# The global term of a fused attention kernel: one split-precision matmul of 96 rows, or a plain fp32 matmul of 32 rows

## The reference

```python
h = einsum('bhid,oi,od->bho', x, weighted_sum, weight)    # (4, 512, 256)
h = concatenate([h, txt], axis=1)                         # (4, 589, 256): 77 rows of text
n = layernorm(h)
gate = sigmoid(relu(n @ gate_w1 + gate_b1) @ gate_w2 + gate_b2)   # 64, then R = 32 columns
glob = gate * (n @ U_w) * cumsum(n @ V_w, axis=1)                 # (4, 589, 32)
h = h + conv3(n, conv_w) + glob @ out_w + out_b                   # out_w is 32 x 256
# then layernorm again, both operands rounded to 8-bit integers, their product, scaled, added to h
```

## Time and profile before

| | before |
|---|---|
| time, median of 3 runs | 128.95 us |
| time of the profiled execution | 129.47 us |
| its span, first to last instruction | 127.7 us |
| PE busy | 109.4 us (86%) |
| DVE busy | 88.2 us (69%) |
| ACT busy | 59.3 us (46%) |
| POOL busy | 49.5 us (39%) |
| mean granted TensorE clock | 0.967 |

### The profile page before, as it was taken

The page is one execution under the profiler, slowest core; times in us unless marked ns, Lnnn a source line. Parts: engine busy times, 40 slices in busy tenths (PEclk is TensorE's granted clock), DMA queues, the critical chain, the costliest instruction groups (busy, mean ns, idle before and its releaser), DMA issues.

```text
span 127.7 us, 1866 instructions
## 1 busy us (share of the span) xinstructions
PE 109.4 (86%) x568; PEld 88.3 (69%) x568; DVE 88.2 (69%) x266; ACT 59.3 (46%) x128; POOL 49.5 (39%) x91
## 2 busy tenths in 40 slices
PE   6169999999999999999979999998995389199960
PEld 6057886687886988788658868866882277099740
DVE  0251440659519688975978898599689999978962
ACT  4000037564632584747247582934485846315520
POOL 2000042002202437171637646360947437416840
PEclk9999999999999999999999999999999959968997
DMA  2999999992000000000022000002020001300014
GB/s 86 253 362 285 397 417 424 424 421 85 0 0 0 0 0 0 8 0 0 0 82 81 1 27 5 0 0 85 0 82 25 0 0 41 124 5 25 0 41 148
DMA packets 5447, 12.55 MB, mean 98 GB/s; under 512 B 471, under 2 KB 3391, under 8 KB 4671
## 3 DMA queue, kind: packets, MB, share of 16 engines
q1 hardware_dynamic: 5151, 11.93, 25.9%
q10 hardware_dynamic: 288, 0.52, 1.4%
HBM read 10.04 MB, written 2.41 MB: 98 GB/s over the span
## 4 chain that ended last, share of the span: by engine, by line
PE 58%; DVE 21%; DMA 8%; issue 3%; ACT 3%; SPq 2%; POOL 2%; DVEq 0%; POOLq 0%
PE h_ps L708 31%; DMA txt_sb<-txt_dram 8%; DVE convT L603 6%; DVE csum L591 5%; PE uvg_ps L766 5%; PE h_ps L790 4%; PE xt_ps L824 3%; PE qt_ps L806 3%; DVE stats L542 3%; DVE tmp L669 3%; PE acc_ps L817 2%; PE h_ps L793 2%; SPq L299 2%; PE xt_ps L752 2%; PE uvg_ps L773 2%
## 5 line engine op out<-in xcount | busy, mean ns | idle before, releaser
L708 PE MATMUL h_ps<-w_tok,x_sb 128*128 128x256 f32 x256 | 64.6, 396 | 3.9 <-DVE w_tok L537 3.9
L708 PEld LDWEIGHTS h_ps<-w_tok,x_sb 128*128 128x128 f32 x256 | 48.3, 198 | 13.1 <-DMA x_sb<-x_dram 4.2
L542 DVE BATCH_NORM_STATS2 stats<-h_ps 128x6 f32<-128x256 f32 (+1 forms) x36 | 13.9, 422 | 12.0 <-PE h_ps L793 6.6
L340 POOL TENSOR_SCALAR rstd<-mv 128x2 f32<-128x2 f32 (+2 forms) x21 | 4.7, 226 | 40.5 <-DVE mv L545 40.0
L378 POOL TENSOR_SCALAR v<-xc,qmul 128x256 f32<-128x256 f32 (+1 forms) x20 | 10.7, 540 | 16.6 <-DVE qmul L647 16.4
L603 DVE SCALAR_TENSOR_TENSOR convT<-xnT,par_sb,convT 128x255 f32<-128x255 f32 (+1 forms) x32 | 16.4, 567 | 0.0
L341 POOL TENSOR_TENSOR rstd<-rstd,exponent 128x2 f32<-128x2 f32 (+2 forms) x21 | 14.9, 711 | 1.7
L494 ACT ACTIVATE xc<-h_ps,nmean 128x256 f32<-128x256 f32 (+1 forms) x20 | 8.6, 469 | 10.7 <-DVE nmean L619 10.7
L470 ACT ACTIVATE glob<-glob 32x256 fp32r<-32x256 f32 (+1 forms) x16 | 7.2, 448 | 11.9 <-POOL glob L352 6.3
L484 ACT ACTIVATE xn<-h_ps,shift,rstd 128x256 f32<-128x256 f32 x16 | 8.2, 563 | 8.7 <-DVE shift L631 8.6
L352 POOL TENSOR_TENSOR glob<-gate,us 32x256 f32<-32x256 f32 x8 | 6.6, 830 | 13.6 <-ACT gate L461 13.6
(11 more groups left out here) (75 smaller groups left out, 141.0 us busy)
## 6 DMA issues: line engine op xcount, KB each, us to landing
x_sb<-x_dram SPq DMA_DIRECT2D x6, 1024.0 KB, 17.2
out_dram<-fin SPq DMA_DIRECT2D x8, 256.0 KB
x_sb<-x_dram SPq DMA_DIRECT2D x4, 256.0 KB, 6.5
x_sb<-x_dram SPq DMA_DIRECT2D x2, 512.0 KB, 9.8
wt_sb<-wt_dram ACTq DMA_DIRECT2D x2, 256.0 KB, 4.7
txt_sb<-txt_dram SPq DMA_DIRECT2D x1, 308.0 KB
out_dram<-fin SPq DMA_DIRECT2D x4, 77.0 KB
par_sb<-par_dram SPq DMA_DIRECT2D x1, 277.0 KB, 10.6
```

The source lines that it names most:

```text
L542: last = nc.vector.bn_stats(stats[0:rows, t, :], src(t))
L708: last = nc.tensor.matmul(h_of(g)[:, t, :], x_sb[:, g, kc, t * P:(t + 1) * P], w_tok[:, kc, :], start=(kc == 0 and t == 0), stop=(kc == KC ...
```

## The change

The matmul of the global term reads `glob` and `outw` as they are, fp32, 32 rows. The rounded copies, the subtraction, both buffers, the type and three semaphores go. `mix` waits for `glob` itself, and GpSimd's wait before it overwrites `glob` is now for the `mix` that read it.

```diff
-        glob3 = sb("glob3", [3 * R, 2, L], F32R)
-        outw3 = sb("outw3", [3 * R, D], F32R)
...
             def gated(g):
                 b, half = divmod(g, HALVES)
                 if half == 0 and b >= 2:
-                    pool.wait_ge(glob_high, 2 * HALVES * (b - 1))
-                    pool.wait_ge(glob_low, HALVES * (b - 1))
+                    pool.wait_ge(mix_done, ITEMS_PER_B * (b - 1))
...
-            def outw_split():
-                act.wait_ge(par_loaded, 16)
-                for n in (0, 1):
-                    nc.scalar.activation(outw3[n * R:(n + 1) * R, :], outw, ACT.Copy).then_inc(outw_high, 1)
...
-                for g in groups(tick, "high"):
-                    b, half = divmod(g, HALVES)
-                    lo, hi = GLOB_RANGES[half]
-                    act.wait_ge(glob_ready, ITEMS_PER_B * b + (ITEMS_PER_B if half == HALVES - 1 else half + 1))
-                    if b >= 2:
-                        act.wait_ge(mix_done, ITEMS_PER_B * (b - 1))
-                    for n in (0, 2):
-                        nc.scalar.activation(glob3[n * R:(n + 1) * R, b % 2, lo:hi], glob[:, b % 2, lo:hi],
-                                             ACT.Copy).then_inc(glob_high, 1)
...
-            def outw_low():
-                dve.wait_ge(outw_high, 2)
-                nc.vector.tensor_tensor(outw3[2 * R:3 * R, :], outw, outw3[0:R, :].bitcast(F32), ALU.subtract)
...
-                for g in groups(tick, "low"):
-                    b, half = divmod(g, HALVES)
-                    lo, hi = GLOB_RANGES[half]
-                    if g == 0:
-                        outw_low()
-                    dve.wait_ge(glob_high, 2 * g + 1)
-                    nc.vector.tensor_tensor(glob3[R:2 * R, b % 2, lo:hi], glob[:, b % 2, lo:hi],
-                                            glob3[0:R, b % 2, lo:hi].bitcast(F32), ALU.subtract).then_inc(glob_low, 1)
...
             def mix(j):
                 b, i, nt, rows = item(j)
                 pe.wait_ge(conv_ready, CB * HALVES * (b + 1))
-                pe.wait_ge(glob_high, 2 * (HALVES * b + min(i + 1, HALVES)))
-                pe.wait_ge(glob_low, HALVES * b + min(i + 1, HALVES))
+                pe.wait_ge(glob_ready, j + 1)
...
-                    last = nc.tensor.matmul(h_item(j)[0:rows, t, :], glob3[:, b % 2, at:at + rows], outw3[:, :],
+                    last = nc.tensor.matmul(h_item(j)[0:rows, t, :], glob[:, b % 2, at:at + rows], outw,
                                             start=False, stop=True, skip_group_check=True)
```

More of the change, by code:

```diff
@@ L7 @@
 F32 = mybir.dt.float32
-F32R = mybir.dt.float32r
 BF16 = mybir.dt.bfloat16
@@ L25 @@
 GROUP_AT = dict(stats=0, rstd=0, shift=1, norm=2, turn=3, move=6, hidden=7, relu=8, sums=8, gates=9,
-                sigmoid=11, gated=10, high=12, low=13, mid=7, tap0=9, tap2=10)
+                sigmoid=11, gated=10, mid=7, tap0=9, tap2=10)
 MIX_AT = ((11, 15, 19), (11, 15, 19), (11, 15, 19), (12, 14, 15))
@@ L33 @@
 GROUP_AT_LAST = dict(stats=0, rstd=0, shift=0, norm=1, turn=4, move=4, hidden=5, relu=8, sums=6,
-                     gates=9, sigmoid=11, gated=11, high=11, low=12, mid=8, tap0=10, tap2=11)
+                     gates=9, sigmoid=11, gated=11, mid=8, tap0=10, tap2=11)
 ITEM_AT_NEXT_TO_LAST = dict(stats=1, rstd=2, centre=1, keep=3, scale=3, round=4, turn=5, ints=6,
@@ L269, in early_fusion_kernel @@
         glob_ready = sem("glob_ready")
-        glob_high = sem("glob_high")
-        glob_low = sem("glob_low")
-        outw_high = sem("outw_high")
         conv_start = sem("conv_start")
@@ L511, in _ @@
                     txt_sigmoid()
-                    outw_split()
                 for g in groups(tick, "mid"):
```

## The result

The changed kernel takes 145.58 us (median of 4 runs, 143.81 to 146.53) against 128.66 us: the ratio is 1.1227, 95% interval 1.1164 to 1.129, some 15.8 us slower. In this document medians are of all runs, while every ratio leaves out the runs more than 1.5% above the fastest of their kernel (here 146.35 and 146.53 us). The forecast was 141.7 us, with a range of 134.2 to 143.5: the direction and the main cost were right, the size was too small. The profiled execution took 143.81 us with a span of 141.7 us, against 129.47 and 127.7 before.

A forecast was written before the change was run, and what follows sets the result against it. PE was taken to bound the kernel, with 58% of the chain. Nineteen tiles at 0.31 us passes plus 0.36 us stall gave 12.7 us on 128.95, so 141.7 us, with a range of 134.2 to 143.5.

The forecast's parts named there:

- The chain and the nineteen tiles: Global matmuls in the mixes: nineteen tiles lie on the chain, each 0.67 us dearer, 12.7 us together.
- Passes 0.31, stall 0.36: Each global-matmul tile on PE: 0.31 us more for two fp32 passes, 0.36 us for a stall around the 32-row matmul.
- The lower bound of the stall: Global matmul on PE: stall of 0, if line 773's 32 output columns and not its 64 rows cause its stall.
- The drain: Skill's rule that changing tiling mode drains TensorE: by it the new 32-row matmuls would pay the stall, taken as 0.36 us.
- The gain on ACT and DVE: Dropped copies (7.2 us of ACT) and subtractions (3.6 us of DVE) lie off the chain: gain 0, bounds 0 and 0.4 us.
- The clock: Half-clock stretch in mixes 9 and 10: about the same length as before, adding 0, bounds 0 and 0.9 us.
- passes only: Rival: the 32-row matmul does not stall, 19 x 0.31 = 5.9 us more, 134.8 us; chance 0.28.
- Loads laid open: Rival: neither weight load of a pair overlaps a matmul, 1.0 us a tile, 19 us more, 148 us; chance 0.06.
- idle time that swallows it: Rival: PE's 7.2 us of waits hide the 5.9 us of passes, 128.2 us; not slower, chance 0.03.

The follow-up runs named there:

- split_bridge: Kernel before, with nine warm matmuls added in PE's wait directly ahead of mix 9; 128.50 us, ratio 0.9999.
- glob128: Changed kernel with glob held in 128 partitions, rows 32 to 127 zero, so the fp32 global matmul has 128 rows; 134.68 us, ratio 1.0464 to the kernel before.
- split32: Kernel before with only the first 32 of the 96 rows given to the global matmul, one pass, copies and subtraction kept; 136.92 us, ratio 1.065.
- plain_bridge: Changed kernel with nine warm matmuls put into PE's wait directly ahead of mix 9; 139.85 us, ratio 1.0907 to the kernel before.
- plain_bridge_again: Changed kernel with the nine warm matmuls ahead of mix 9, run again beside the unedited one; 139.46 us, ratio 1.082 to the kernel before.
- plain_again: Changed kernel, unedited, run again for more times and clocks; 144.99 us, ratio 1.117 to the kernel before.
- plain_first: Kernel before with the 32-row fp32 matmul in batches 0 to 2 only, 96 rows in the last, copies and subtraction kept; 137.52 us, ratio 1.0735.
- plain_last: Kernel before with the 32-row fp32 matmul in the last batch's five tiles only, copies and subtraction kept; 134.02 us, no ratio, runs 130.29 to 137.43.
- glob64: Changed kernel with zero rows added so the fp32 global matmul has 64 rows; 143.38 us, ratio 1.1149 to the kernel before.
- gates_full: Kernel before with the gates' matmul (line 773) of groups 0 to 6 zero-filled to 128 by 128, in the transposes' bank; 128.16 us, ratio 0.996.

## Why the prediction was wrong

- *The chain and the nineteen tiles*: right for the first fourteen. Counted from the first statistics, those behind mix 2 are late by 3.34 us (3.4 forecast); those behind mix 7 begin at 104.35 us (105.1 forecast), and of the difference of 0.75 us, 0.56 is the earlier start of this execution, which is luck. The five tiles of the last batch were priced too high: at full clock they cost 2.2 us and not 3.35, because PE had idle time to give there (0.80 us ahead of `q_turn` in split_bridge).
- *Passes 0.31, stall 0.36*: right, each by itself, in glob128 and split32. The lower bound of the stall, 0 if only the narrow output of line 773 caused it, is excluded: 64 rows with 128 output rows stall, and 128 rows with 32 output rows as well. 96 and 77 do not.
- *The drain*. The rule of the Trainium skill, TensorEngine Tiling (Array Packing), section Key Properties, agrees with these traces for 32 and 64 rows by 128 and for 128 rows by 32 output rows, which stall. What is shown is the price; that it is a drain was not measured.
- *The gain on ACT and DVE, 0 (bounds 0 and 0.4)*: nothing speaks against it. The stretch from the statistics behind mix 7 to mix 9 is 0.71 us shorter in the profiled execution. But other traces of the changed kernel have 15.91 to 16.17 us there (plain_bridge, plain_bridge_again, plain_again), and those where copies and subtraction stay 15.75 to 16.28 (plain_first, plain_last, split32). So the 0.71 lies within what executions differ by, and it too is luck.
- *The clock*: this step failed. I wrote of a stretch "of about the same length" that "adds nothing", with bounds of 0 and 0.9 us. The stretch became three times as long, 10.2 us for 3.4, and costs 3.9 us more than before in the profiled execution. The price of a tile was applied to work that no longer had the clock at which it was read. The upper end of the range came from that bound, and so it lay too low. The profiled 143.81 us lies only 1.6 us above the forecast of 142.2, since the misses have both signs: 3.9 us for the clock were missing, 1.1 too much stood for the last tiles, and the two differences of this execution, 0.71 and 0.56, took off the rest.
- *The rivals*: passes only is what glob128 does, and not the change. Loads laid open and idle time that swallows it did not occur.

What stays open: whether it is the few rows or the stalls around them that keep the clock low; every run with one had the other. Also what the stretch at half clock ahead of mix 9 costs: it lasts 3.4 us in some traces and 6.8 in others (plain_again, plain_bridge_again, glob64), and the time up to mix 9 does not follow it clearly. And whether the 0.36 us splits into loads and way in and out as I assumed.

## What to carry to other kernels

A matmul whose rows or output rows are few is not cheap: look in the timeline of the weight loads for loads that start only with their matmul, and try zero rows up to the full array before anything else; here 128 rows instead of 32 were some 10 us faster for the same product. A cost per instruction read at full clock holds only while the clock does: where the work ahead is thin and the clock already low, ask what the slower work will do to it, and put both lengths of the stretch into the range. And an operation moved earlier starts its successors earlier too, on engines where they may disturb the one that matters.

No version here beats the kernel before by more than the 0.5% that can be told; gates_full, at 0.996 (0.9923 to 0.9998), comes nearest.

## What the runs showed of the hardware

- A matmul of 32 or 64 rows between full ones with 128 output rows costs 0.36 us beyond its passes (32 rows in plain fp32 and in one pass of the rounded type, 64 rows in plain fp32): 0.19 in the matmul, 0.15 in two transposes behind it or 0.19 in the `tok` instructions. One of 96 or 77 rows costs none.
- A filled matmul with zeros takes the time of any full one: 0.43 us for two fp32 instructions of 256 columns.
- The clock fell to 1.2 GHz while PE was occupied, 2 us behind a wait of only 0.94 us: in plain_bridge it went to 0.50 between mixes 9 and 10, with 2.56 us of busy time from 119.0 to 122.5 us.
- The same PE instructions, from mix 9 to the last addition, took 14.61, 17.75, 19.27 and 20.65 us with 0, 6.8, 10.2 and 13.7 us at 1.2 GHz among them.
- DVE's four last taps took 1.99 us with POOL idle for most of them, and 3.01 us beside a GpSimd addition that was itself lengthened, 1.60 us against a mean of 1.26 for its shape in gates_full.
